# One transposing DMA of twelve blocks a visit instead of one of four and one of eight, with new instruction orders

## What is computed

```python
x = x + einsum(z @ R - z, U)                 # layer 0: U from a QR of P, R = expm of a skew matrix from cond
for layer in (L1, L2, L3):
    h = modulate(norm(x), shift_msa, scale_msa)
    q, k, v = split(h @ W_qkv + b)           # L3 also normalises q and k per head
    att = softmax(einsum('bhqd,bhkd->bhqk', q * 9 ** -0.5, k))
    x = x + gate_msa * (einsum('bhqk,bhkd->bhqd', att, v) @ W_proj + b)
    h = modulate(norm(x), shift_mlp, scale_mlp)
    x = x + gate_mlp * (gelu(h @ W_fc1 + b) @ W_fc2 + b)
```

## Time and profile before

| | |
|---|---|
| median of 3 runs | 363.49 us (363.12 to 363.57) |
| the profiled execution | 363.12 us; its span on the core 361.2 us, mean granted TensorE clock 0.934 of full speed |
| first part, to the first layer's input | 0 to 113 us |
| slots 0 to 3, filling | 113 to 151 us |
| pairs of slots in layers 0 and 1 | 17.6 us each |
| pairs of slots in layer 2 | 20.6 and 20.7 us |
| last 29.2 us | 332 to 361.2 us |

### The profile page before, as it was taken

The page is one execution under the profiler, slowest core; times in us unless marked ns, Lnnn a source line. Parts: engine busy times, 40 slices in busy tenths (PEclk is TensorE's granted clock), DMA queues, the critical chain, the costliest instruction groups (busy, mean ns, idle before and its releaser), DMA issues.

```text
span 361.2 us, 10726 instructions
## 1 busy us (share of the span) xinstructions
PE 308.4 (85%) x3494; PEld 211.6 (59%) x3502; DVE 293.4 (81%) x1511; ACT 207.2 (57%) x460; POOL 166.2 (46%) x536
## 2 busy tenths in 40 slices
PE   1969983983668998799999999999999998989896
PEld 0924721472124455486878777777666675766675
DVE  4999999999995678787888888787989888887632
ACT  4145110244011365688888887888686867768552
POOL 5424332356553322535354545454646646452442
PEclk9987655697699999999999999999999999999999
DMA  4797400039300233223222222222023222223101
GB/s 147 185 255 234 126 1 0 4 80 291 117 1 0 45 60 76 45 45 46 45 44 48 45 45 48 44 47 46 15 45 32 45 47 45 45 41 37 34 16 34
DMA packets 48735, 23.58 MB, mean 65 GB/s; under 512 B 40186, under 2 KB 47198, under 8 KB 48552
## 3 DMA queue, kind: packets, MB, share of 16 engines
q1 hardware_dynamic: 48680, 22.89, 27.8%
HBM read 12.82 MB, written 0.62 MB: 37 GB/s over the span
## 4 chain that ended last, share of the span: by engine, by line
PE 42%; DVE 39%; issue 8%; DMA 4%; POOL 3%; SPq 1%; ACT 1%; POOLq 0%; DVEq 0%
PE ps L1016 34%; DMA skw_r<-brief 4%; DVE grow L1647 4%; DVE nmax L1976 3%; DVE top L1702 3%; DVE trow L1647 3%; PE ps L1415 3%; DVE beta L1681 3%; DVE den L1687 2%; DVE tfac L1695 2%; DVE lead L1669 2%; DVE late L1669 2%; PE ps L1309 1%; DVE gfac L1663 1%; DVE grec L1659 1%
## 5 line engine op out<-in xcount | busy, mean ns | idle before, releaser
L1976 DVE TENSOR_REDUCE nmax<-ps 128x4 f32<-128x512 f32 x96 | 63.4, 683 | 11.7 <-PE ps L1016 11.4
L796 ACT ACTIVATE skw_t<-ps 128x512 f32<-128x512 f32 x96 | 52.0, 595 | 14.8 <-PE ps L1016 14.2
L448 POOL TENSOR_TENSOR root<-grow,half 32x1 f32<-32x1 f32 x64 | 34.6, 542 | 54.0 <-DVE grow L1647 53.6
L1016 PE MATMUL ps<-skw_r 54*128 54x128 bf16 x768 | 43.5, 217 | 4.7 <-DMA skw_r<-brief 2.3
L1016 PEld LDWEIGHTS ps<-skw_r 54*128 54x128 bf16 x768 | 30.4, 94 | 20.8 <-issue 11.5
L1016 PE MATMUL ps<-mT_t,fc1w_t 128*128 128x256 f32 (+1 forms) x130 | 36.0, 379 | 0.0
L1016 PE MATMUL ps<-fc2w,skw_r 128*128 128x144 f32 (+1 forms) x240 | 34.7, 292 | 0.0
L1016 PE MATMUL ps<-sel,identb 128*128 128x512 bf16 x83 | 23.7, 404 | 9.6 <-DVE grow L1647 8.6
L1016 PEld LDWEIGHTS ps<-fc2w,skw_r 128*128 128x128 f32 (+1 forms) x240 | 30.8, 190 | 1.6 <-issue 0.2
L1016 PE MATMUL ps<-nmT,sel 64*128 64x128 bf16 x384 | 27.6, 216 | 0.0
L813 ACT ACT_TABLE_LOAD x21 | 26.9, 1283 | 0.4
(11 more groups left out here) (273 smaller groups left out, 815.4 us busy)
## 6 DMA issues: line engine op xcount, KB each, us to landing
gmod<-spread_mods SPq DMA_DIRECT2D x3, 1408.0 KB, 13.2
adaw_t<-in_ada SPq DMA_DIRECT2D x3, 432.0 KB
tails<-in_tail SPq DMA_DIRECT2D x3, 427.1 KB
skw_t<-in_skw SPq DMA_DIRECT2D x1, 1024.0 KB
fc1w_t<-in_fc SPq DMA_DIRECT2D x3, 320.0 KB
fc2w<-in_fc SPq DMA_DIRECT2D x3, 288.0 KB
skw_r<-brief SPq DMA_TRANSPOSE x48, 3.1
qkvw_t<-in_qkv SPq DMA_DIRECT2D x3, 216.0 KB
```

What stands on the lines that cost most here:

```text
L448: g.tensor_tensor(root[:, p, j:j + 1], grow[:, i % 4, 0:1], half[:], ALU.pow).then_inc(root_ready, 1)
L796: a.activation(prob[g].rearrange("p i t -> p (i t)"), ps[:, 2 + g % 2, :], ACT.Exp, scale=SCALE).then_inc(prob_ready, 1)
L1016: return pe.matmul(o, lhsT, rhs, start=start, stop=stop, skip_group_check=True)
L1976: d.tensor_reduce(nmax[:, v % 2, first:first + 7:2], ps[:, 6 + g % 2, :].rearrange("p (i t) -> p i t", i=4), AX_X, ALU.max, negate=True).t ...
```

## The change

Three things are changed. First, the DMAs L375 and L376 become one of twelve blocks, and the semaphore `keys_turned` goes: `scores(v, 0)` and ACT's `first` wait for `turned` alone.

```diff
-                sp.dma_start_transpose(both_turned[h][:, 12:16, :], both_parts[h][:, 12 * T:16 * T]).then_inc(keys_turned[h], 16)
-                sp.dma_start_transpose(both_turned[h][:, 4:12, :], both_parts[h][:, 4 * T:12 * T]).then_inc(turned[h], 16)
+                sp.dma_start_transpose(both_turned[h][:, 4:16, :], both_parts[h][:, 4 * T:16 * T]).then_inc(turned[h], 16)
...
             def scores(v, g):
                 if v == 0:
-                    stay_warm(8)
+                    stay_warm(6 - 2 * g)
                 if v == 1:
                     stay_warm(1 + g)
                 if g == 0:
                     pe.wait_ge(qT_ready, v + 1)
-                    pe.wait_ge(keys_turned[v % 2], 16 * (v // 2 + 1))
-                else:
                     pe.wait_ge(turned[v % 2], 16 * (v // 2 + 1))
```

Second, of the 16 useless products around the first scores 8 stay: 6 ahead of `scores(0, 0)` and 2 ahead of `scores(0, 2)`. Third, all four engines' orders are written anew. One line of each kind, from DVE's table for an even slot of layers 0 and 1 (it has 20 rows) and POOL's for the same:

```diff
                     visit_at(second_parts, slot + 1, start=1)
+                    visit_at(third_parts, slot + 1, start=1)
                     visit_at(next_normal, slot + 2, start=2)
-                    visit_at(third_parts, slot + 1, start=1)
...
+                    visit_at(attention_add, slot - 3)
-                    visit_at(attention_add, slot - 2)
```

More of the change, by code:

```diff
@@ L632, in _ @@
+                    visit_at(inverse_norms, slot, start=2 * B)
+                    pair_at(second_deviation, slot, 4)
                     pair_at(mlp_add, slot, 6)
@@ L1484, in _ @@
                     visit_at(o_turn, slot - 2)
-                    visit_at(last_fc1_main, slot - 3, start=LAST)
                     visit_at(last_fc1_tail, slot - 3, start=LAST)
+                    visit_at(scores, slot, 0)
+                    visit_at(last_products, slot - 4, start=LAST)
                     pair_at(h2_turn, slot, 4)
-                    visit_at(parts_turn, slot)
+                    visit_at(proj, slot - 2)
+                    visit_at(h_turn, slot + 1, start=2)
+                    visit_at(scores_T, slot - 1, 2)
@@ new lines, in _ @@
+                    visit_at(qkv, slot + 1, start=1)
+                    visit_at(pv, slot - 1, 0)
+                    visit_at(pv, slot - 1, 1)
+                    pair_at(fc1, slot, 4, 0)
+                    visit_at(pv, slot - 1, 2)
+                    visit_at(scores, slot, 2)
+                    visit_at(pv, slot - 1, 3)
+                    visit_at(parts_turn, slot)
+                    visit_at(last_turn, slot - 2, start=LAST)
+                elif slot >= VISITS - 1 and slot % 2 == 1:
+                    pair_at(fc1, slot, 5, 1)
+                    visit_at(o_back, slot - 2)
+                    pair_at(fc1, slot, 5, 2)
+                    visit_at(o_turn, slot - 2)
+                    visit_at(parts_turn, slot)
+                    visit_at(last_tail_turn, slot - 3, start=LAST)
+                    visit_at(h_turn, slot + 1, start=2)
+                    visit_at(max_turn, slot - 1)
+                    visit_at(qkv, slot + 1, start=1)
+                    visit_at(proj, slot - 2)
+                    visit_at(scores_T, slot - 1, 0)
+                    pair_at(fc2, slot, 5, 0)
@@ L2116, in _ @@
                     visit_at(input_stats, slot + 3, start=2)
-                    visit_at(next_normal, slot + 2, start=2)
-                    visit_at(input_means, slot + 3, start=2)
                     visit_at(residue, slot + 1, start=1)
@@ L2141, in _ @@
                     visit_at(maxima, slot, 1)
-                    visit_at(gated, slot - 2)
-                    visit_at(residue, slot + 1, start=1)
-                    visit_at(second_parts, slot + 1, start=1)
-                    pair_at(mlp_out, slot, 5)
-                    visit_at(maxima, slot, 2)
-                    visit_at(maxima, slot, 3)
-                    visit_at(input_means, slot + 3, start=2)
-                    visit_at(max_high, slot)
-                    visit_at(max_low, slot)
@@ L2196, in _ @@
+                    visit_at(maxima, slot, 2)
+                    pair_at(second_input, slot, 3)
                     visit_at(maxima, slot, 3)
@@ L2209, in _ @@
                     visit_at(norm_sum, slot + 1, start=2 * B)
+                    visit_at(gated, slot - 2)
                     visit_at(norm_floor, slot + 1, start=2 * B)
-                    visit_at(gated, slot - 2)
+                    visit_at(input_means, slot + 3, start=2)
                     visit_at(norm_seed, slot + 1, start=2 * B)
```

390 lines of the change are left out of this document (188 added, 202 removed).

## The result

The changed kernel takes 369.53 us (median of four runs, 368.06 to 372.18) against 363.31; the ratio is 1.0175, with a 95% interval of 1.0143 to 1.0207. Timed once more beside other kernels it took 370.2 us against 363.32, a ratio of 1.0183 (1.0144 to 1.0223). The forecast was 365.2 us (+1.7) within 360.7 to 368.2: the sign came out as the likeliest case had it, the size is 3.7 to 4 times as large, and the time is above the range. The profiled execution took 370.76 us, its span is 369.0.

The account below looks back on a forecast made before the run. PE was taken as full in layers 0 and 1, and waits between PE and DVE as setting layer 2's pace; 1.1 + 0 + 1.4 - 0.8 = +1.7 us gave 365.2 us, range 360.7 to 368.2.

Parts of the forecast that it names:

- the likeliest case: Whole kernel: the forecast's own sum, slower at 365.2 us, own range 364.3 to 367, chance 0.42.
- the fill: Start of the kernel, 113 to 151 us: first scores wait for all twelve blocks, +1.1 us, between -0.3 and +3.
- full pairs: Slot pairs of layers 0 and 1: the new order widens the transfers' margins, PE's work is unchanged, 17.6 us stay, 0.
- layer 2: Four pairs of layer 2: late odd-slot scores and new DVE order cost 0.35 us a pair, +1.4, bounds -3 to +3.
- the end: Last stretch: proj(21) ahead of scores_T(22, 0) brings -0.6, o_T(23) ahead of a gelu -0.2, together -0.8 us.
- the falls of the clock: Rival: with fewer useless products PE idles 2 us before the first scores and the clock falls, 368 us, chance 0.02.
- the late landings: Rival: late transfers hold up all scores of a visit, 0.9 us each in three layer 2 visits, 367.7 us, chance 0.08.
- each transfer's margin: Full pairs, visits 8 and 9: with landing at 3.9 us, the new order leaves margins of about 1.1 and 0.7 us.
- The transfer's part: In the fill: scores(0, 0) waits for twelve blocks, so scores(0, 2) comes at 126.55 instead of 125.65, +0.9 us.
- The orders' part: In the fill, slot 1: residue(2) now lies between two maxima and holds up scores(1, 2) by up to 0.35 us.
- The -0.15 from visit 3: In the fill: the shift falls partly into visit 3's existing wait for a late transfer, giving back 0.15 us.
- the transfer's lateness in odd slots: Layer 2, odd slots: first scores come 0.5 us late for the transfer, of which DVE sees 0.2.

Follow-up runs that it names:

- e3: The changed kernel with the two transfers and 8 + 8 useless products put back, so only the orders differ from the kernel before: 366.92 us, ratio 1.0096.
- e1: The kernel before with only the one transfer of twelve blocks, for which scores(v, 0) waits; old orders and 8 + 8 useless products stay: 371.7 us, ratio 1.0178.
- e2: The kernel before with only the useless products around the first scores cut from 8 + 8 to 6 + 2: 362.62 us, ratio 0.9996.
- e6: The kernel before with its two transfers, but scores(v, 0) waits for both: 405.94 us, ratio 1.1029 of the two shortest runs alone.
- e14: The kernel before with all engines' new orders in slots 2 to 14, PE's odd slots as before, and 6 + 2 useless products: 362.27 us, ratio 0.9968.
- e10: The changed kernel with 15 useless products instead of 6 ahead of scores(0, 0), and 4 each ahead of parts_turn(3) and o_turn(1): 373.83 us, ratio 1.0263.
- e4: The changed kernel with 15 useless products instead of 6 ahead of scores(0, 0): 371.79 us, ratio 1.02.
- e13: The changed kernel with the old pair of transfers for visits 16 to 23 (layer 2): 368.38 us, ratio 1.0143.
- e7: The kernel before with one transfer of twelve blocks in layers 0 and 1 and the two transfers in layer 2: 366.9 us, ratio 1.0089.
- e5: The kernel before with the changed kernel's orders of the last slots, from slot 23 on, on all four engines: 362.73 us against 362.75, ratio 0.9993.

## Why the prediction was wrong

The two profiles of the changed kernel, cut at m = 1, 5 and 8, put beside each term of the sum what came (from m = 5 to 8 are three of layer 2's four pairs):

| term | forecast | first profile | second profile |
|---|---|---|---|
| the fill | +1.1 | +4.70 | +2.10 |
| full pairs | 0 | +1.22 | +1.24 |
| layer 2 | +1.4 | +1.66 | +4.04 |
| the end | -0.8 | +0.2 | +0.2 |

No term was too high, and the two largest misses are the two rivals that had 0.02 and 0.08: the falls of the clock in the first profile's fill, the late landings in the second's layer 2.

**The full pairs: 0.** This step failed. "PE's work is the same, so 17.6 us stay" holds for the products, not for their time: PE was busy 17.38 of 17.60 us, so a growth of its busy time is paid at once, but for the 0.2 us of room. It grew by 0.45 us a pair, by the order alone, for 0.32 us of time. From m = 1 to m = 5 that is +1.2 us in e3. The step looked at each transfer's margin, which was right: `scores(8, 0)` and `scores(9, 0)` did not wait, 5.13 and 4.18 us behind the issue with a landing of 3.7 (the margin forecast as 0.7 adds up to 0.57 by its own numbers, and came out at 0.5). It looked at this and not at what stands ahead of and behind each group of products.

**The fill: +1.1.** The mechanism was right, the size low. The transfer's part was 0.9: e1's first turn of the maxima came 1.05 us later (129.17 against 128.12). The orders' part was 0.35. In e3 m = 1 is at +1.04, of which 0.79 came with the late first keys, so the runs do not show that this part was too low. The -0.15 from visit 3 can't be told apart. What the sum left out is the clock, next.

**The clock, priced as a rival at 0.02.** It fell in the fill, where a window at 99 us with PE busy 1.64 of 3 us had been taken as evidence that it would not. PE was idle for 1.36 us in that window and is idle for 2.03 us ahead of the first scores, in one piece. The Trainium skill's warning (TensorE: Matmul & The Clock Gate, "HAM oscillation"), which the prediction set aside for that row, agrees with what came at the first fall, behind a wait for the DMA. Of the five profiles with 6 + 2 products four have a fall near 125 us (all but e2); of the eleven with 8 + 8 or more only e6 has one. So the eight products removed were not without use. The length of the idle time alone does not tell which: e14 fell behind 0.82 and 1.01 us, e1 and e3, with 8 + 8, held behind 1.61 and 1.46. The price of the first fall is read from the start of `scores(0, 0)` to the first turn of the maxima. In e10, where the clock held, this is 4.32 us, as in e4:

```profile
125.84 0.40 PE L1018 MATMUL ps<-skw_r 54*128 54x128 bf16 x8 [1.14 <-issue]
130.16 0.22 PE L1387 MATMUL ps<-identb,nmp 128*128 128x128 bf16 x1
```

In the changed kernel it is 5.95 us (124.44 to 130.39), the second time 5.61, in e13 5.47: the fall cost 1.1 to 1.6 us there. In the first profile it made the next step, from the first to the second turn of the maxima, 5.69 us instead of 5.39, 0.3 more. The second fall, in one of the two profiles, made the step from the third to the fourth 8.83 us instead of 6.21, 2.6 more. That is the difference between the two fills, and likely part of the scatter of 368 to 372 us. Together the two falls cost the first profile some 4.5 us. The rival had 2.8 us for one fall and a chance of 0.02, which was far too low. That the medians of e4 and e10 do not give this back was measured and not explained; in the profiles of these two, late landings stand in the falls' place.

**Layer 2: +1.4.** The first profile has 1.66 us for three pairs, the forecast 1.05 (0.35 each). The orders alone cost 0.43 us a pair (1.30 in e3) and had been given 0.15; the transfer's lateness in odd slots had been given 0.2 and added 0.12. PE did wait ahead of the odd visits' first scores as forecast (0.35, 0.88 and 0.28 us). What the sum left out is the rival "late landings hit the first scores", named with 0.9 us a landing (three of them are 2.7 us, for which it wrote 2.5) and a chance of 0.08. In the changed orders the stretch from m = 5 to m = 8 was longer than before by

| profile | us | landings of 4.9 us or more in visits 16 to 22 |
|---|---|---|
| e3, e13 (two transfers) | 1.30, 1.62 | the first scores waited for none |
| changed | 1.66 | none |
| e10 | 3.47 | 2 |
| changed, second time | 4.04 | 2 |
| e4 (a run well above its median) | 6.06 | 4 |

which is some 0.9 to 1.2 us a landing, and it is not rare: with one transfer in layer 2, under these orders and in e1, five profiles have 0, 2, 2, 4 and 2. Where the clock fell behind the landing, it cost more: in e1 the three pairs of layer 2 lost 3.3 us (late landing and fall), 0.8 (neither) and 1.8 (late landing alone), in e7 0.0, 2.6 (both) and 0.0. The rival's price was near the truth for the landing itself, its chance far too low. The earlier trace rows had shown the cause. Before, late landings belonged mostly to the eight-block transfer (4.5 to 5.0 us in five of 24 visits; once, at 166.9, the four blocks took 4.3), and an eight-block wait that no one needed early was made the wait of all.

**The end: -0.8.** Failed. `proj(21)` and its `gated` did come earlier in e5 (331.42 and 332.19 against 332.24 and 333.01, of which 0.5 us was there by m = 8), but the last turn of the maxima came 0.42 us earlier (338.49 against 338.91) and the end 0.3: the gain was gone within 7 us, and e5 shows 0. Both steps were taken for parts of the path that ends last. The prediction named the wait of 1.09 us for the product and did not follow the chain from there to the end; at which handover the gain was lost was not traced.

**The sum.** By the medians: orders 3.7, one transfer with fewer products 2.6 to 3.3 on top, together 6.2 to 6.9 us. The parts do not simply add. Under the old orders the one transfer alone costs as much as the whole change (ratios 1.0178, and 1.0175 and 1.0183). So beside two transfers the new orders cost 3.7 us, and beside one they cost nothing that can be told. One place where they give it back is seen: in layer 2's odd visits they bring the issue forward, and PE idles 0.28 to 0.88 us ahead of the first scores instead of e1's 0.85 to 1.24.

**Open.** Why a landing is late was not tried. What the trace shows is the course of one, in 40 slices of the 5.5 us from the issue of visit 16's transfer in the second profile, with the packets of each queue under it:

```profile
DMA  0000000019999999999999514000000000000000
GB/s 0 0 0 0 0 0 0 0 22 190 220 214 210 210 212 210 209 210 218 194 201 211 96 21 132 0 0 0 0 0 0 0 0 0 0 0 0 0 0 0
q1 hardware_dynamic: 1568, 0.39, 37.8%
q8 instruction: 1, 0.02, 1.0%
```

The data is through after some 3.4 us, with one packet of instructions in the same stretch, and the landing is seen 2 us later. In e4 each of the four late landings has such a packet between issue and landing, and the three transfers of visits 17, 19 and 21, which landed after 3.6 to 4.1 us, have none of that queue. In all sixteen profiles together 48 of 616 transfers of these blocks landed 4.5 us or more after their issue, and each of the 48 had such a packet in that time. But so had 144 that landed sooner, many of them on time, and a longer wait has more room for one, so this is a trail, not a cause shown.

## What to carry to other kernels

Joining two transfers saves an issue, but its price is set by who needed the first of them: look at the distance from issue to first use in every visit, at the latest landing and not the median, since one wait for everything exposes all of it. Where TensorE is full, count busy time and not products when the order changes: one group of ten between other neighbours cost 0.2 us here. Products that seem useless in front of a wait should be judged by the granted clock without them, in several profiles: one of five without them showed no fall.

## What the runs showed of the hardware

- A wait for a transfer costs from its margin on. First scores that could begin 3.7 us behind the issue cost the settled full pairs nothing (e1). At 4.4 us (e6) they cost 1.35 us a pair where the clock held, 1.0 of it as idle time of PE ahead of them; with late landings and eight falls of the clock behind 113 us in its profile, that kernel's runs came out 36 to 46 us longer.
- Eight useless products of 0.24 us each were removed from around the first wait. With 6 + 2 the clock fell near 125 us in four of five profiles, with 8 + 8 or 15 + 2 in one of eleven. A fall there cost 1.1 to 1.6 us up to the first turn of the maxima.
- A transposing DMA of twelve blocks is issued in 1.43 and lands in 3.7 us; the same transfer took 4.9 to 5.4 us in some visits, and which ones differed between executions of one kernel.
- A late landing that held up all scores of a visit cost a pair of layer 2 some 0.9 to 1.2 us. With a fall of the clock behind it (e1 at 268.5, e7 at 297.2) the pair came out 3.3 and 2.6 us longer than before.
- The same ten float32 products took 1.39 us behind `proj`, 1.50 behind the bfloat16 scores and 1.49 behind the short float32 products of `pv`.
